# Spectra stored by mode and then image, placed by GpSimd, and mixing weights asked for three steps ahead

## What is computed

```
h = concat(grid, x) @ P_w + P_b                      # 128 images, 32 channels, 64 x 64
for i in range(4):
    h_ft = rfft2(h)                                  # only 16 x 16 modes are used
    out_modes = einsum('bixy,ioxy->boxy', h_ft[:, :, :16, :16], spec_wr[i] + 1j * spec_wi[i])
    spec = irfft2(out_modes, s=(64, 64))
    h = leaky(spec + conv3x3(h, conv_w[i]) + conv_b[i])
out = leaky(h @ Q1_w + Q1_b) @ Q2_w + Q2_b
```

## Time and profile before

| | us |
|---|---|
| median of three runs | 7531.51 |
| the profiled run | 7536.45 |
| its span, first to last instruction | 7534.4 |
| TensorE busy | 6726.4 (89%) |
| VectorE busy | 4995.7 (66%) |
| ScalarE busy | 2567.0 (34%) |
| GpSimd busy | 61.3 (1%) |
| mean granted TensorE clock | 0.961 |

### The profile page before, as it was taken

The page is one execution under the profiler, slowest core; times in us unless marked ns, Lnnn a source line. Parts: engine busy times, 40 slices in busy tenths (PEclk is TensorE's granted clock), DMA queues, the critical chain, the costliest instruction groups (busy, mean ns, idle before and its releaser), DMA issues. The chain is left out here.

```text
span 7534.4 us, 262144 instructions
## 1 busy us (share of the span) xinstructions
PE 6726.4 (89%) x107382; PEld 3991.5 (53%) x107382; DVE 4995.7 (66%) x7931; ACT 2567.0 (34%) x4418; POOL 61.3 (1%) x47
## 2 busy tenths in 40 slices
PE   5699998999999899999989999758888888888888
PEld 4466666666666666666654444334434444344443
DVE  3599995777777477777667777664545555455454
ACT  1244442333333233333223333233343333433333
POOL 1000000000000000000000000000000000000000
PEclk8899998999999899999999999879999999999999
DMA  6444444444444444444432222200000000000000
GB/s 155 113 124 129 125 124 134 125 124 118 123 124 110 138 118 124 124 118 123 117 100 77 77 76 75 86 6 1 3 1 3 3 1 3 2 2 3 1 3 2
DMA packets 655549, 568.39 MB, mean 75 GB/s; under 512 B 328096, under 2 KB 527904, under 8 KB 649126
## 3 DMA queue, kind: packets, MB, share of 16 engines
q1 hardware_dynamic: 655176, 563.43, 28.2%
HBM read 315.77 MB, written 247.61 MB: 75 GB/s over the span
## 5 line engine op out<-in xcount | busy, mean ns | idle before, releaser
L548 PE MATMUL abank<-inv_basis,mode_tile 128*32 128x128 f32 x32768 | 1013.6, 276 | 94.6 <-DMA mode_tile<-m_img 66.4
L594 PE MATMUL zbank<-rows_in,conv_taps 64*32 64x512 f32 (+1 forms) x18432 | 1049.7, 588 | 0.0
L548 PEld LDWEIGHTS abank<-inv_basis,mode_tile 128*32 128x32 f32 x32768 | 877.3, 111 | 269.4 <-issue 269.4
L954 DVE SCALAR_TENSOR_TENSOR rows_out<-zbank,conv_bias,work 128x1024 f32<-128x1024 f32 x512 | 633.7, 1279 | 516.9 <-PE zbank L603 504.9
L816 ACT ACTIVATE turned<-tbank 128x1024 f32<-128x1024 f32 x400 | 410.2, 1026 | 1550.9 <-PE tbank L617 1550.9
L810 ACT ACTIVATE inv_copy<-abank 128x1024 f32<-128x1024 f32 x512 | 524.4, 1024 | 776.4 <-PE abank L548 776.4
L632 PE MATMUL zbank<-fwd_basis,turned 128*64 128x128 f32 x12288 | 760.2, 277 | 19.9 <-ACT turned L816 13.1
L930 DVE TENSOR_TENSOR work<-inv_copy 128x512 f32<-128x512 f32 x1024 | 653.6, 684 | 164.1 <-ACT inv_copy L810 163.8
L632 PEld LDWEIGHTS zbank<-fwd_basis,turned 128*64 128x64 f32 x12288 | 668.6, 137 | 97.7 <-issue 97.7
L603 PE MATMUL zbank<-rows_in,conv_taps 32*32 32x512 f32 (+1 forms) x18432 | 702.5, 593 | 0.0
L594 PEld LDWEIGHTS zbank<-rows_in,conv_taps 64*32 64x32 f32 x18432 | 329.5, 106 | 583.0 <-issue 583.0
(11 more groups left out here) (367 smaller groups left out, 7091.2 us busy)
## 6 DMA issues: line engine op xcount, KB each, us to landing
h_rows<-rows_out SPq DMA_DIRECT2D x768, 256.0 KB, 4.1
rows_in<-h_rows SPq DMA_DIRECT2D x384, 512.0 KB, 4.9
m_img<-rows_out SPq DMA_DIRECT2D x32, 1024.0 KB, 5.3
mode_tile<-m_img SPq DMA_DIRECT2D x512, 64.0 KB, 3.1
rows_in<-x_pad SPq DMA_DIRECT2D x384, 48.7 KB
rows_out<-x_pad SPq DMA_DIRECT2D x384, 48.7 KB
tokens<-spectra SPq DMA_DIRECT2D x512, 4.0 KB
weights<-in_weights SPq DMA_DIRECT2D x1, 6060.0 KB, 19.5
```

The source lines that it names most:

```text
L548: last = nc.tensor.matmul(ab[32 * p:32 * p + 32, s, 128 * k:128 * k + 128], mode_tile[u][:, k, a, :], inv[:, k, s, 128 * p:128 * p + 128], ...
L594: nc.tensor.matmul(section(zb[32 * p:32 * p + 32, 2 * a + so, :])[:, :, :, out], conv_t[part, dx, so, :], moving(part, p, 0, src), start=( ...
L954: nc.vector.scalar_tensor_tensor(out=rows_out[u][:, half].rearrange("p (s x) -> p s x", s=2), in0=zb[:, 2 * a:2 * a + 2, :], scalar=conv_b ...
```

## The change

`spectra` is now seen with the mode outside and the image inside, so that the 128 images of a mode are packed. ScalarE no longer writes it in the pair loop: it copies the 256 columns of `gb` with one activation to a new tile `placed`, for which it first waits until GpSimd has emptied it (`g_placed`), and GpSimd makes the eight copies of 32x128 from `placed` into `g_img`. These now write with a step of 128 elements, and so do the copies of the expansion in layer 0. TensorE waits for `g_placed` at the start of a mixing stage. In `sp_mix` the weights of step `a + 3` are asked for in round `a`, right behind the store of step `a - 1`; in layer 0 those of steps 1 to 3 are asked for before the first round.

```diff
@@ -72,7 +72,8 @@
 
         PADDED = PIX + 2 * COLS
         spectra = sb("spectra", [128, IMGS * 128])
-        g_img = spectra[:].rearrange("p (n m) -> p n m", n=IMGS)
+        g_img = spectra[:].rearrange("p (m n) -> p n m", n=IMGS)
+        placed = sb("placed", [128, 2 * MX * MY // 2])
         rows_flat = sb("rows_in", [128, 2 * PADDED])
         rows_in = [rows_flat[:, PADDED * u:PADDED * u + PADDED] for u in range(2)]
         rows_flat_out = sb("rows_out", [128, 2 * PIX + 4160])
@@ -164,6 +165,7 @@
         cols_folded = sem("cols_folded")
         fwd_done = sem("fwd_done")
         g_ready = sem("g_ready")
+        g_placed = sem("g_placed")
         h_stored = [sem(f"h_stored{u}") for u in range(2)]
         g_stored = sem("g_stored")
         q1_done = sem("q1_done")
@@ -424,13 +426,16 @@
 
         def sp_mix(sp, l, kind):
 
+            if kind == "first":
+                for a in range(1, 4):
+                    sp_load_weights(sp, l, a)
             for a in range(8):
-                if a >= 4 or (a >= 1 and kind == "first"):
-                    sp_load_weights(sp, l, a)
                 if kind == "first" and a in (1, 2, 3, 4):
                     sp_slot(sp, a - 1)
                 if a >= 1:
                     sp_store_mixed(sp, l, a - 1)
+                if 1 <= a <= 4:
+                    sp_load_weights(sp, l, a + 3)
                 if kind == "first" and a >= 4:
                     sp_late_constants(sp, a - 4)
             if kind == "first":
@@ -531,6 +536,26 @@
             nc.gpsimd.memset(rows_flat[:, MODES * ET:], 0.0).then_inc(zeroed, 1)
             nc.gpsimd.memset(rows_flat_out[:], 0.0).then_inc(zeroed, 1)
             nc.gpsimd.memset(uv_flat[0], 0.0).then_inc(zeroed, 1)
+
+            def place(n, l):
+
+                pool.wait_ge(g_ready, ET + PAIRS * l + n + 1)
+                pool.nop(nofuse=True)
+                for x in range(2):
+                    for a in range(2):
+                        at = 64 * x + 32 * a
+                        for r in range(2):
+                            part = slice(64 * x + 32 * r, 64 * x + 32 * r + 32)
+                            image = g_img[part, 2 * n + a, :] if isinstance(n, int) else \
+                                g_img[part, bass.ds(2 * n + a, 1), :].rearrange("p n m -> p (n m)")
+                            last = nc.gpsimd.tensor_copy(image, placed[at:at + 32, 128 * r:128 * r + 128])
+                last.then_inc(g_placed, 1)
+
+            with looped(pool, 0, PAIRS) as n:
+                place(n, 0)
+            with pool.Fori(1, LAST) as l:
+                with looped(pool, 0, PAIRS) as n:
+                    place(n, l)
 
 
         section = lambda ap: ap.rearrange("c (h j w) -> c h j w", h=2, w=COLS)
@@ -752,6 +777,7 @@
                 else:
                     pe_need(pe, z_free, 2 * PAIRS * l)
                     pe_need(pe, g_ready, ET + PAIRS * l)
+                    pe_need(pe, g_placed, PAIRS * l)
                     pe_need(pe, a_copied, 2 * PAIRS * l)
                     pe_need(pe, turned_copied, 2 * (ET + PAIRS * l))
                 for a in range(8):
@@ -819,16 +845,8 @@
             def modes_copy(u, n, l, i):
 
                 act.wait_ge(fwd_done, 2 * (ET + PAIRS * l + n) + 2)
-                act.nop(nofuse=True)
-                for x in range(2):
-                    for a in range(2):
-                        at = 64 * x + 32 * a
-                        for r in range(2):
-                            part = slice(64 * x + 32 * r, 64 * x + 32 * r + 32)
-                            image = g_img[part, 2 * n + a, :] if isinstance(n, int) else \
-                                g_img[part, bass.ds(2 * n + a, 1), :].rearrange("p n m -> p (n m)")
-                            last = nc.scalar.activation(image, gb[at:at + 32, 128 * r:128 * r + 128], ACT.Identity)
-                last.then_inc(g_ready, 1)
+                need(act, g_placed, PAIRS * l + n)
+                nc.scalar.activation(placed[:], gb[:, 0:256], ACT.Identity).then_inc(g_ready, 1)
 
             def scaled(m, r):
 
@@ -892,8 +910,9 @@
                     for i in range(8):
                         act.wait_ge(expanded, i + 1)
                         for g in range(2):
-                            at = 128 * (32 * g + 4 * i)
-                            last = nc.scalar.activation(spectra[:, at:at + CH], xbank[i % 2][g], ACT.Identity)
+                            at = 32 * g + 4 * i
+                            last = nc.scalar.activation(g_img[:, at:at + 4, :], xbank[i % 2][g].rearrange("p (n m) -> p n m", n=4),
+                                                        ACT.Identity)
                         last.then_inc(expand_act, 1)
                 for a in range(8):
                     act.wait_ge(mix_done, 8 * l + a + 1)
@@ -1052,8 +1071,8 @@
                     for i in range(8):
                         dve.wait_ge(expanded, i + 1)
                         for g in range(2, 4):
-                            at = 128 * (32 * g + 4 * i)
-                            last = nc.vector.tensor_copy(spectra[:, at:at + CH], xbank[i % 2][g])
+                            at = 32 * g + 4 * i
+                            last = nc.vector.tensor_copy(g_img[:, at:at + 4, :], xbank[i % 2][g].rearrange("p (n m) -> p n m", n=4))
                         last.then_inc(expand_dve, 1)
                 else:
                     need(dve, z_done, PAIRS * l)
```

## The result

The changed kernel took 7411.65, 7423.94, 7423.99 and 7444.6 us, median 7423.97; the kernel before, run beside it, 7531.88 (four runs). The ratio is 0.9852, 95% interval 0.9838 to 0.9866: 108 us faster. In a later comparison it was 7422.51 against 7549.36 (five and nine runs), ratio 0.9833, interval 0.9814 to 0.9852. The forecast was 7458, so the forecast gain of 73 us was too small by a third; the result lies in the stated range (7383 to 7530), and 1 us outside the forecast's own range (7425 to 7490).

What follows compares the result with a forecast made beforehand. VectorE was taken to bound layer 0, TensorE layers 1 and 2, with nothing full in the mixing stages. From 7531.5 us, -84, -39, -13 and +1 (-135) with +62 for VectorE gave -73: 7458 us, range 7383 to 7530.

Steps and rivals of the forecast that it cites:

- Step 1: Mixing, layers 1 to 3: packed loads let a step's 32 records take 3.7 us instead of 7.0 at full clock.
- Step 2: Mixing, layers 1 to 3: weights three steps ahead end the 7.79 us wait; with packed loads, 28 us a layer, -84.
- other sum, by bytes alone: Mixing, layers 1 to 3: 12.6 MB at 349 GB/s take 36 us from the first store, plus 2.
- The starts: End of a layer: GpSimd's placing in series before mixing, +0.3 us (-0.7 to +2.6) at three starts, +1.
- Step 3: Layer 0 mixing: weights ahead of SyncE's constants, -42 us, less 3 for the expansion's strided writes, net -39.
- ends of 0 and 9: Layer 0 expansion: strided writes by ScalarE and VectorE cost 0 to 9 us over eight steps, 3 taken.
- Step 4: Pair loop, layers 1 and 2: one modes copy frees the bank earlier, 0.10 to 0.11 us per pair, -13.
- Step 5: Pair loop: GpSimd's eight placing copies take 0.25 us each, 2.0 in all, and the engine keeps up.
- a sign that it is wrong: GpSimd's placing copies taking over 0.5 us would show the prediction wrong.
- Step 6: Layer 0 pairs: GpSimd's copies delay VectorE's two-input instructions, 4 x 0.25 = 1.0 us a pair, +62.
- rival of no disturbance: Layer 0 pairs: GpSimd reads beside VectorE at no cost; -135 us in all, 7396 us; chance 0.28.
- slower rival: Layer 0 pairs: all GpSimd copies land in VectorE's chain, 3.2 us per pair, +198, total 7594 us; chance 0.14.

Runs made afterwards that it cites:

- weights-alone run: The kernel before with only the new order of SyncE's weight loads, layout and ScalarE's eight copies unchanged: 7466.56 us, ratio 0.9902.
- edit to runs of four: The changed kernel with layer 0's expansion copies going modes outside, four images inside, so each write is four packed elements: 7428.79 us.
- memset run: The changed kernel with GpSimd's eight copies per pair in layer 0 replaced by memsets of the same shape and step: 7394.87 us (one run).

## Why the prediction was right or wrong

**What bounds the kernel.** The reading of the stages held: gains came where TensorE waited for weights or SyncE's queue was long, losses where VectorE was full. One gain has no term in the prediction, the clock behind the first read (below).

**Step 1, packed stationary operand: right.** The loads take at full clock what the earlier trace rows said. That it was neither the clock nor late weights is shown by the weights-alone run: with both in order a step stays at 7.0 us.

**Step 2, weights ahead: right in kind, short in size.** First matmul to first read: forecast 49 us, measured 45.9, 47.2 and 47.4, so -90 in three layers for -84. The mis-sized term is the step at the DMA's pace. I gave the last four steps 4.5 us each by their bytes, 18; they took 15.3 in layer 1 (1186.98 to 1202.3), three of them at TensorE's own 3.6 and 3.7: the weights of a = 4 and 5 were there when VectorE came to them, and it waited 0.41 and 1.50 us for the next two. The prediction's other sum, by bytes alone, came out better than the one it took: 38 us from the first store to the first read, measured 38.9, 39.5 and 39.5. Another 6 us of the 97 come from a term that the prediction put at nothing: the stretch from the first read to the first row, 18.1 instead of 20.0 us, because the two inverse transforms in it, the second above all, ran at a higher granted clock. The starts gave -1 for +1. So -97 instead of -83.

**Step 3, layer 0: right, with errors that offset each other.** Last store 198.72 for a forecast of 194.3 and 3 us for the expansion, so 1.4 us late; its landing 14.6 us later instead of 17.8, so 3.2 early. The expansion cost 6.1 us, not 3: copies of 2.47 us became its bound, which I had thought hidden behind TensorE. It stayed within its ends of 0 and 9. From the first matmul of the expansion to the first of the mixing it is 15.9 us before, 22.0 in after and 16.8 with the edit to runs of four. That edit takes back 5.2 of the 6.1 us, with copies as long as before the change: that much is the strided write. The rest stays open.

**Step 4: right.** 12.4 us for 13, convolution 5.33 us in the steady pair, and 1140.7 us for the pairs of layers 1 and 2 in every kernel that gives the bank back early, in either layout.

**Step 5: copy mis-sized, without effect.** Not 0.25 us but 0.39 alone and up to 5.4 beside VectorE, 0.87 in the mean. The prediction had named copies of over 0.5 us as a sign that it is wrong. They are over it, yet the sign misled: a copy is long because it is held or alternates, and the first costs VectorE nothing, the second 0.09 us. Nobody waits for it in the pair loop. The starts of the mixing moved by +1.7, -2.3 and -0.7 us.

**Step 6 is the step that failed: 62 us forecast, 17.4 measured.** I had a copy slip in whole at each boundary, four times 0.25 us a pair. In fact in half of the pairs GpSimd waits and VectorE loses only what is left over when L983 starts (0.19 us), and in the others a copy costs each of four VectorE instructions 0.09 us and not its own length. That VectorE pays at all for GpSimd's read is right, as the memset run shows; how the two engines share was wrong. The rival of no disturbance was wrong too: it would have needed copies that don't read, which the memset run shows at 7394.87 us, or copies short enough to fit beside L973, as in the old layout, or four instead of eight. The slower rival is far off: 0.28 us per pair, where it needed 2.2. The range's lower end came from no disturbance; the result lies between that case and the forecast. The error of 34 us on the median is this term (45 us), the mixing with the stretch behind it (14) and layer 0's start (1), less 25 us: 8 that the profile lost outside the terms (layer 3's pairs and the blocks) and 17 by which the profiled runs differ more than the medians do. That the total error is under the 60 us of the terms is luck.

**What stays open.** By what rule the first copy's start selects the way of sharing: its place beside L949 separates the two in all of layer 0's pairs, but in layers 1 and 2, where it begins beside a longer instruction, no copy is held. Open too is why VectorE's price is just 0.09 us, and why the granted clock behind the first read is full in one stage and half in another. And whether the blocks' spread of 25 us has a cause: no run here touches them.

## What to carry to other kernels

Two halves of a change that act on one stage should be costed together and apart: here -42 and -19 became -97, since each removes the bound that the other leaves. Work moved to GpSimd cost VectorE time only where both read SBUF, and it mattered only in the stage where VectorE was the bound. There it went away when the copies left over fitted beside VectorE's PSUM reads: shorten them (packed writes) or share them out until they do. A load moved ahead in a full DMA queue delays what then stands behind it; look for who is next in that queue before moving it.

## What the runs showed of the hardware

- A GpSimd copy of 32x128 floats SBUF to SBUF takes 0.285 us with packed writes and 0.39 to 0.41 with a step of 512 bytes; a memset with that step 0.33.
- Beside VectorE instructions with two SBUF inputs such a copy is either held until 0.14 to 0.29 us behind the last of an unbroken run (up to 5.42 us; VectorE 1.22) or takes as long as one of them (1.2 us; VectorE 1.30). In layer 0 the first copies held began 0.10 to 0.25 us inside a 128x512 instruction, those not held 2 to 78 ns ahead of it; in layers 1 and 2 none was held.
- Sixteen loads of a 128x128 stationary operand with a step of 512 bytes take 3.59 us and packed 1.87, at the full granted clock; back to back a mixing step of 32 records comes every 7.0 and every 3.6 us.
- A copy of 128x512 floats from PSUM by ScalarE or VectorE, two in a row: 1.09 and 1.29 us packed or in runs of four, 2.47 with a step of 512 bytes between the elements written. Reading PSUM with a step of 512 bytes costs nothing here.
